# A new order of finds, sorts, deals and indirect transfers, with a sixth of each unit's slots weighted on GpSimd, in a graph attention layer with sparse gathers

## The reference

```python
h = jnp.maximum(_layernorm(x, axis=-1), 0.0)        # x: 8192 x 256
hp = (h @ W.T).reshape(n, 8, 32)
attn = s_src[:, None, :] + s_dst[None, :, :] + adj[:, :, None] * We[:, 0] + be
attn = jnp.where((adj > 0)[:, :, None], attn, -jnp.inf)
attn = softmax(leaky_relu(attn, 0.2), axis=1)
out = x + einsum('ijh,jhd->ihd', attn, hp) + h @ Wr.T + br
```

## Time and profile before

| | us |
|---|---|
| median of 3 timed runs | 2473.1 (2469.73 to 2473.41) |
| span of the profiled execution | 2707.2 |
| VectorE busy | 2058.7 (76%) |
| GpSimd busy | 1627.7 (60%) |
| ScalarE busy | 1264.6 (47%) |
| TensorE busy | 1104.5 (41%) |
| mean rate of all DMA | 180 GB/s |

### The profile page before, as it was taken

How to read it: one execution, slowest core, us unless ns; L and a number is a source line. 1 busy time by engine, 2 the same in 40 slices (tenths; PEclk the granted TensorE clock), 3 DMA queues, 4 the chain that set the end, 5 groups by cost and what they waited for, 6 DMA issues and landing times.

```text
span 2707.2 us, 24949 instructions
## 1 busy us (share of the span) xinstructions
PE 1104.5 (41%) x3781; PEld 826.0 (31%) x3782; DVE 2058.7 (76%) x5510; ACT 1264.6 (47%) x5256; POOL 1627.7 (60%) x1928
## 2 busy tenths in 40 slices
PE   4676003331150237534363336346245344245244
PEld 3554002221140226322152215225134234234123
DVE  5897819983974899757289848989989999997312
ACT  2332002262121336846585556466475464466376
POOL 5444671477265677677537763675774764763774
PEclk9988556665575667666566656666666666666667
DMA  6446752674644676766358764876877787782332
GB/s 151 152 139 212 223 124 81 189 214 120 200 139 141 208 209 192 214 164 189 106 173 251 200 182 152 236 250 194 254 240 226 240 248 232 237 242 55 85 91 57
DMA packets 166650, 488.40 MB, mean 180 GB/s; under 512 B 35744, under 2 KB 54200, under 8 KB 166280
## 3 DMA queue, kind: packets, MB, share of 16 engines
q1 hardware_dynamic: 86088, 278.11, 31.7%
q0 software_dynamic: 80400, 208.74, 29.4%
HBM read 449.88 MB, written 36.83 MB: 180 GB/s over the span
## 4 chain that ended last, share of the span: by engine, by line
DVE 29%; issue 25%; ACT 12%; DMA 12%; POOL 12%; another core or an unknown queue 5%; PE 3%; SPq 1%; POOLq 0%; DVEq 0%; ACTq 0%
ACT arena L1173 10%; POOL arena L596 10%; DVE work L758 8%; DMA arena<-table,arena 7%; DVE work L747 7%; DVE arena L909 2%; DMA out_dram<-w_all,arena 2%; DVE work L804 2%; DVE work L801 2%; DVE work L803 2%; DVE work L800 1%; DMA adj_sb<-in_adj_dram 1%; PE banks L1327 1%; ACT pre L1158 1%
## 5 line engine op out<-in xcount | busy, mean ns | idle before, releaser
L596 POOL DMA_INDIRECT arena<-table,arena x1253 | 1306.0, 1042 | 624.6 <-issue 392.0
L1173 ACT ACTIVATE arena<-arena,prob 128x32 f32<-128x32 f32 x4456 | 1000.4, 308 | 249.5 <-issue 229.4
L1305 PE MATMUL banks<-arena,ident 128*128 128x256 f32 x1392 | 448.3, 495 | 1109.1 <-DVE arena L909 887.1
L1305 PEld LDWEIGHTS banks<-arena,ident 128*128 128x128 f32 x1392 | 350.9, 258 | 1206.1 <-issue 902.5
L747 DVE FIND_INDEX8 work<-work,adj_sb 128x8 uint32<-128x502 f32 (+56 forms) x775 | 670.7, 868 | 0.0
L758 DVE MAX8 work<-adj_sb 128x8 f32<-128x502 f32 (+56 forms) x775 | 659.3, 858 | 0.0
L1311 PE MATMUL banks<-arena,ident 128*128 128x256 f32 x1114 | 381.8, 472 | 376.2 <-remote 255.6
L1168 ACT ACTIVATE prob<-pre 128x120 f32<-128x120 f32 (+21 forms) x67 | 21.7, 323 | 943.2 <-DVE pre L893 710.5
L1311 PEld LDWEIGHTS banks<-arena,ident 128*128 128x128 f32 x1114 | 226.3, 223 | 516.6 <-remote 303.8
L909 DVE TENSOR_TENSOR arena<-arena,prob 128x768 f32<-128x768 f32 (+8 forms) x166 | 200.7, 1258 | 0.0
L1158 ACT ACTIVATE pre<-arena,we_all 128x13 f32<-128x13 f32 (+27 forms) x536 | 170.4, 407 | 51.4 <-DMA arena<-lists 31.6
(11 more groups left out here) (130 smaller groups left out, 1088.0 us busy)
## 6 DMA issues: line engine op xcount, KB each, us to landing
adj_sb<-in_adj_dram SPq DMA_DIRECT2D x505, 512.0 KB, 15.3
arena<-table,arena POOLq DMA_INDIRECT x1253
table<-arena POOLq DMA_DIRECT2D x32, 264.0 KB, 2.6
arena<-in_x_dram SPq DMA_DIRECT2D x32, 256.0 KB, 2.8
resid<-arena POOLq DMA_DIRECT2D x32, 256.0 KB, 2.6
out_dram<-arena POOLq DMA_DIRECT2D x32, 256.0 KB, 2.8
adj_sb<-in_adj_dram SPq DMA_DIRECT2D x1, 1536.0 KB, 22.6
lists<-arena,rank POOLq DMA_INDIRECT x67
```

Of the source, the lines that this page charges most:

```text
L596: pool.indirect_dma_start(gath[:, un.slot(k), :], None, table[:, :], bass.IndirectOffsetOnAxis(ap=rec[:, k, 0:1], axis=0), bounds_check=N ...
L1173: last = s.activation(g, g, ACT.Copy, scale=prob[:, b, k * H + h:k * H + h + 1])
L1305: last = m.matmul(ps_sum[:, u % 2, :], ident[:, :], gath[:, un.slot(k), 0:HD], start=(k == 0), stop=False)
```

## The change

- **Finds:** `FOUND` is now a table of points with steps between them: one find more in step 0, the same from unit 1 to 11, and fewer from unit 12 on (51 instead of 53 at unit 40, 59 instead of 61 at unit 48). The last find is in step 60.
- **Groups:** the last group of 8 becomes two of 4; in all 1262 slots instead of 1253. The deals of groups 4 to 8 move by one to two units; for groups 6, 7 and 8 the deal and the load are now behind the same gather (units 34, 42, 50), ahead of the group's first unit.
- **Homes:** three homes for lists instead of two, with a width for each.
- **Scan and sort:** FIND_INDEX8 comes two segments behind MAX8 instead of one; the low and high halves of the sort wait on semaphores of their own.
- **Indirect DMAs** (gathers, stores, deals) have no `bounds_check`.
- **Weights:** ScalarE takes 2K//5 slots (479 in all instead of 557), GpSimd K//6 from unit 12 on (107 in all), VectorE the rest (676 instead of 696). GpSimd's order is now gather(u), weight(u-2), store(u-3). TensorE adds GpSimd's slots last, and ScalarE's exponentials of unit u wait for GpSimd's weights of unit u-2.

```diff
-          (56, (20, 13, 11, 10, 9, 8, 7, 6)))
+          (56, (20, 11, 9, 8)),
+          (60, (18, 11, 9, 7)))
-FOUND = (7, 9, 10, 11, 14, 16, 18, 20, 21, 22)
-LEAD = 13
+FOUND = ((0, 8), (1, 9), (2, 10), (3, 11), (4, 14), (5, 16), (6, 18), (7, 20), (11, 24), (40, 51), (48, 59), (60, 67))
+HOMES = 3
+POOL_FROM = 12
...
-        self.act_slots = K // 2 if K < 18 else 10 if K < 20 or K > 38 else 14 if K < 32 else 16
+        self.act_slots = 2 * K // 5
+        self.pool_slots = K // 6 if u >= POOL_FROM else 0
...
-                        bass.IndirectOffsetOnAxis(ap=rec[:, k, 0:1], axis=0),
-                        bounds_check=N + PAD - 1, oob_is_err=False).then_inc(lane, 16)
+                        bass.IndirectOffsetOnAxis(ap=rec[:, k, 0:1], axis=0)).then_inc(lane, 16)
+
+            def weight(un):
+
+                n, first = un.pool_slots, un.K - un.act_slots - un.pool_slots
+                pool.wait_ge(S["exped"], un.u + 1)
+                for k, at, n in un.slots(first, first + n):
+                    gv = gath[:, at:at + n, 0:HD].rearrange("p k (h d) -> p k h d", d=D)
+                    pb = prob[:, un.u % 2, k * H:(k + n) * H].rearrange("p (k h) -> p k h", h=H)
+                    last = nc.gpsimd.tensor_tensor(gv, gv, pb.unsqueeze(3).to_broadcast([P, n, H, D]), ALU.mult)
+                last.then_inc(S["pool_weighted"], 1)
...
             for un in units:
                 gather(un)
+                if un.u - 2 >= POOL_FROM:
+                    weight(units[un.u - 2])
                 if un.u >= LATE:
                     store(units[un.u - LATE])
...
+            for un in units[-2:]:
+                weight(un)
...
                     v.max(val8[:, 8 * s:8 * s + 8], a[:, bounds[s]:bounds[s + 1]]).then_inc(S["maxed"], 1)
-                    if s:
-                        index(s - 1)
+                    if s >= 2:
+                        index(s - 2)
                 if end == so.segs:
+                    index(so.segs - 2)
                     index(so.segs - 1)
...
+                for keys_of, top, done in ((kl, sl, S["sorted_lo"]), (kh, sh, S["sorted_hi"])):
+                    if m:
+                        dve.wait_ge(done, sorted_before[c] + m - (c if done is S["sorted_lo"] else 0))
+                    if m % 2 == 0:
+                        v.max(top, keys_of).then_inc(done, 1)
+                    else:
+                        v.match_replace(keys_of, top, keys_of, 0.0).then_inc(done, 1)
...
+                if u - 2 >= POOL_FROM:
+                    act.wait_ge(S["pool_weighted"], u - 2 - POOL_FROM + 1)
...
+                if un.pool_slots:
+                    pe.wait_ge(S["pool_weighted"], u - POOL_FROM + 1)
+                for n in range(un.pool_slots):
+                    k = K - un.act_slots - un.pool_slots + n
+                    last = m.matmul(ps_sum[:, u % 2, :], ident[:, :], gath[:, un.slot(k), 0:HD],
+                                    start=False, stop=(n == un.pool_slots - 1))
                 last.then_inc(S["tile_sum"], 1)
```

More of the change, by code:

```diff
@@ L81 @@
 VMAX = 8 * max([n for n, _ in SEGS.values()] + [len(b) - 1 for b in WINDOW_SEGS])
-WIDE = max(len(ks) * (HEAD + 2 * ks[0]) for ks in LISTS)
+WIDES = [max(len(ks) * (HEAD + 2 * ks[0]) for ks in LISTS[i::HOMES]) for i in range(HOMES)]
 VALID = max(len(ks) * ks[0] for ks in LISTS)
@@ L153, in plan @@
             units.append(Unit(len(units), K, group, i))
-    found = [FOUND[u] if u < len(FOUND) else min(len(sources), u + LEAD) for u in range(len(units))]
+    found = []
+    for u in range(len(units)):
+        (u0, f0), (u1, f1) = next(((a, b) for a, b in zip(FOUND, FOUND[1:]) if a[0] <= u < b[0]), (FOUND[-1], FOUND[-1]))
+        found.append(f0 + (f1 - f0) * (u - u0) // max(1, u1 - u0))
     for group in groups[1:]:
@@ L171, in plan @@
                 owner[un.slot(k)] = ("part_sum", part_sums + n + 1)
-        for k in range(un.K - un.act_slots, un.K):
+        for k in range(un.K - un.act_slots - un.pool_slots, un.K):
             owner[un.slot(k)] = ("tile_sum", un.u + 1)
+        assert not un.u > POOL_FROM or all(
+            not free or free[0] == "part_sum" and free[1] <= units[un.u - 2].parts_before or free[0] == "tile_sum" and free[1] <= un.u - 2
+            for free in un.free_at)
         part_sums += un.parts
@@ L252, in gat_kernel @@
         adj_sb = sb("adj_sb", [P, 2, N])
-        arena = sb("arena", [P, GSLOTS * ROW + 4 * WIDE])
+        arena = sb("arena", [P, GSLOTS * ROW + 2 * sum(WIDES)])
         gath = arena[:, 0:GSLOTS * ROW].rearrange("p (k r) -> p k r", r=ROW)
-        stage, dealt = (arena[:, GSLOTS * ROW + i * 2 * WIDE:GSLOTS * ROW + (i + 1) * 2 * WIDE].rearrange(
-            "p (b w) -> p b w", b=2) for i in range(2))
+        homes = [GSLOTS * ROW + sum(WIDES[:i]) for i in range(HOMES)]
+        stage, dealt = ([arena[:, at + i * sum(WIDES):at + i * sum(WIDES) + width] for at, width in zip(homes, WIDES)]
+                        for i in range(2))
         work = sb("work", [P, max(5 * VMAX + 4 * KMAX, 2 * TILES * D)])
@@ L282, in gat_kernel @@
         rank_f = sb("rank_f", [P, GMAX])
[L283 removed]
+        rank = sb("rank", [P, HOMES, GMAX], U32)
         lower = sb("lower", [P, P])
@@ L394, in record @@
         def record(un):
-            return dealt[:, un.group.g % 2, un.place * un.group.W:(un.place + 1) * un.group.W]
+            return dealt[un.group.g % HOMES][:, un.place * un.group.W:(un.place + 1) * un.group.W]
         def staged(so):
-            return stage[:, so.group.g % 2, so.place * so.group.W:(so.place + 1) * so.group.W]
+            return stage[so.group.g % HOMES][:, so.place * so.group.W:(so.place + 1) * so.group.W]
         def pairs(rec, K):
@@ L625, in deal @@
                     pool.indirect_dma_start(
-                        lists[group.g][:, :], bass.IndirectOffsetOnAxis(ap=rank[:, group.g % 2, i:i + 1], axis=0),
-                        stage[:, group.g % 2, i * group.W:(i + 1) * group.W], None,
-                        bounds_check=group.n * P - 1, oob_is_err=False).then_inc(lane, 16)
+                        lists[group.g][:, :], bass.IndirectOffsetOnAxis(ap=rank[:, group.g % HOMES, i:i + 1], axis=0),
+                        stage[group.g % HOMES][:, i * group.W:(i + 1) * group.W], None).then_inc(lane, 16)
             def load_dealt(group):
                 landed(pool, group.deal_seq + group.n)
-                if group.g >= 2:
-                    before = groups[group.g - 2]
+                if group.g >= HOMES:
+                    before = groups[group.g - HOMES]
                     landed(pool, units[before.first + before.n - 1].store_seq + (2 if before.t0 is None else 1))
@@ L812, in decode @@
                 t, K, rec = so.t, so.K, staged(so)
-                if so.place == 0 and so.group.g >= 2:
-                    before = groups[so.group.g - 2]
+                if so.place == 0 and so.group.g >= HOMES:
+                    before = groups[so.group.g - HOMES]
                     landed(dve, before.deal_seq + before.n)
                 pv = pairs(rec, K).bitcast(U32)
-                dve.wait_ge(S["sorted_"], sorted_before[c] + 2 * so.rounds)
+                dve.wait_ge(S["sorted_lo"], sorted_before[c] - c + 2 * so.rounds - 1)
+                dve.wait_ge(S["sorted_hi"], sorted_before[c] + 2 * so.rounds)
                 v.tensor_scalar(pv[:, :, 0], slot_lo[:, 0:K], JBITS, None, ALU.logical_shift_right)
@@ L1311, in tile_sums @@
                     last = m.matmul(ps_sum[:, u % 2, :], ident[:, :], gath[:, un.slot(k), 0:HD],
-                                    start=False, stop=(k == K - 1))
+                                    start=False, stop=(k == K - 1 and not un.pool_slots))
+                if un.pool_slots:
[4 more added lines that the diff above has]
+                                    start=False, stop=(n == un.pool_slots - 1))
                 last.then_inc(S["tile_sum"], 1)
```

37 lines of the change are left out of this document (14 added, 23 removed).

## The result

The changed kernel takes **2569.1 us** (median of 4 runs, 2567.38 to 2573.05), the kernel before on the same chip 2473.3 (2469.73 to 2476.31): a ratio of 1.0395, with an interval of 1.0379 to 1.0410. It is 96 us slower. I had forecast 2552, a range of 2400 to 2620, and slower. Its profiled execution took 2571.4 us, so this profile can be read as it stands.

The account below looks back on a forecast made before the run. It took VectorE's own work plus its waits to set the end, with GpSimd's gathers bounding 815 to 1334 us. Terms -6 + 157 + 22 - 12 - 27 - 60 + 22 - 17 = +79 on 2473.1 gave 2552 us, range 2400 to 2620.

Parts of the forecast that it names:

- item 4: Sort halves on two semaphores, indices two segments behind, three homes for lists: 0, as VectorE's operations follow without gaps.
- the new order: Lower found counts, last find in step 60: tail 155 instead of 229.6 us, taken as -60; find no longer hidden +22.
- transfers without checks: Indirect transfers at 1.25 us instead of 1.30, over some 340 in the GpSimd-bound stretch: -17.
- shares and weighting as such: Part of item 1: VectorE's 20 fewer slots -6, ScalarE waits replaced -27.
- the lock: weight(u-2) queued behind gather(u), so evacuate(u-2) waits: +157 at group edges, +22 at the start, -12 for replaced gather waits.
- The price at group edges: Behind place() in groups 4 to 8, VectorE waits for deals, loads, gathers and weighting before evacuating: +157 together.
- item 1: GpSimd's weighting from unit 12 on and the order it brings: -6, +157, +22, -12, -27.
- about 155 us behind the last find: Sign for the forecast: a tail of that length, instead of 229.6 us counted from 2477.6.
- ScalarE waits nearly gone: Sign for the forecast: VectorE's waits for ScalarE nearly disappear; the sum subtracted 27 for them.
- (a): Rival: indirect transfers become much cheaper, 1.00 us or less each, so 2399 us, faster; chance 0.20.
- (b): Rival: the order at group edges is covered after all, so item 1's 157 isn't there: 2395 us; chance 0.12.
- (c): Rival: GpSimd's multiplications hold VectorE up or the other way round, at most 68 us again, 2620; chance 0.08.

Follow-up runs that it names:

- the undisturbed one: The kernel before, no edit, profiled a second time, without the first profile's odd spells of waiting: 2477.3 us in a single run, span 2475.6.
- the finds placed anew: Changed kernel with a new FOUND table (more finds by units 6 to 12): 2407.8 us weighting ahead of gathers, 2440.8 behind, 2393.6 without GpSimd weighting.
- the best run: Changed kernel with a new FOUND table (more finds by units 6 to 12) and no weighting on GpSimd: 2393.6 us, ratio 0.9673.

## Why the prediction was right, and where it was not

The runs form a chain from the kernel before to the changed one, one part at a time: 2475 without checks 2420, with item 4 2411, with the shares and GpSimd's weighting ahead 2430, with the new order 2471, with the weighting behind the gathers 2569.

| part | in my sum | measured |
|---|---|---|
| transfers without checks | -17 | -55 (-61 on the changed kernel) |
| item 4 | 0 | -10, intervals overlap |
| shares and weighting as such | -6 - 27 = -33 | +19 |
| the new order | -60 + 22 = -38 | +41 |
| the lock | 157 + 22 - 12 = +167 | +98 (+52 in the old order) |
| together | +79 | +93 |

The measured parts sum to 93 from a base of 2475 to 2476; the result itself is 96 over its own base of 2473. The prices hold for the parts added in this order: the runs show others for the lock and the weighting where the rest differs.

The sign is right, and so is the mechanism of the largest term, the weighting's place behind the gathers. That the forecast came within 17 us is luck: four of five terms are off by 35 us or more, against each other, and the new order, which I had as a gain of 38, is a loss of 41. The steps:

**The price at group edges** was right. I worked out 22 for the start (step 13) and then 10, 23, 3, 38, 27, 28, 28. The trace has 24.9 and then 8.9, 18.8, 4.2, 30.8, 23.9, 25.5, 25.5, with two of 2.0 and 6.6 besides: 171 against 179. Most edges are a little cheaper, as a load and a landing took less than taken from the earlier trace rows (the lists were there 3.50 us after the load, not 6.3).

**What the lock replaces** was the failed step of item 1. I subtracted 12.3 from the earlier trace rows, that is, the gather waits of the kernel before behind 1345. But the lock stands in the new order, and there VectorE waits 280 us for gathers over the whole kernel, of which the lock takes 130 over. Then 214.5 - 4.2 - 130 + 20 (L919, 49.8 against 30.0) = 100, and the medians say 98. Here a wait moved one find ahead cost only what it exceeded the old wait by.

**The new order** failed by a term that I put at nothing, not by those that I had. Behind the last find I had 155 - 32 = 123 us; the changed kernel took 119.5 (2451.9 to 2571.4). (The 155 is counted from the old last find, so my sign "about 155 us behind the last find" was put wrongly.) Against the run with the old order the tail is 94 us shorter (215.6 to 122.1). What it pays is a last find that comes 131 us later (2343 instead of 2211.8): 27 are the six steps from 54 to 60 at 4.5 (I had counted seven), 21 the find that is no longer hidden (22 predicted), 71 are waits for gathers between 1150 and 2211, which I didn't have, and 12 are left over. These waits stand behind the deals, which the lower counts of finds push from three units ahead of a group to right ahead of its first gathers. I had reckoned such edges only for the lock; without the lock the same gathers are late for the scores.

**The transfers.** The period, 1.25, was right. The row that I took it by, the register MOVE of 29 ns, is gone from the trace, but what got shorter is the transfer itself, by 50 ns. That my guess of 1.25 hit it is partly luck. The stretch that they bound was wrong: the earlier trace rows were taken from 815 on, and the gathers ahead of it, and those up to 1580, weren't looked at.

**ScalarE's waits.** I subtracted 27 for them from the execution with the spells. In the undisturbed one they are 26.5, and in the changed kernel they rise to 49.8. The new order raises them: with the same shares and the weighting ahead they are 10.1 in the old order and 30.0 in the new, and the lock takes them to 49.8. Of the things that I said would show the forecast right, "ScalarE waits nearly gone" failed.

**Rivals.** (a) fell: the gap of 0.30 stays. (b) fell: the lumps are there. (c) fell as a price of 68 us, as one slot instead of K//6 costs the same, but what it is about is there. In the changed kernel's timeline of VectorE and GpSimd, an operation of VectorE beside a multiplication of GpSimd, and the same one elsewhere:

```profile
1606.31 1.92 POOL L617 TENSOR_TENSOR arena<-arena,prob 128x1024 f32<-128x1024 f32 x1
1606.61 1.70 DVE L792 SCALAR_TENSOR_TENSOR work<-work,seg_base 128x56 uint32<-128x56 uint32 x1
...
2382.69 0.22 DVE L792 SCALAR_TENSOR_TENSOR work<-work,seg_base 128x56 uint32<-128x56 uint32 x1
```

It takes 1.70 us instead of 0.22 and ends 0.08 us after GpSimd's. What the Trainium skill says in "GPSIMD Engine Reference", section 1 Specifications, of SBUF interfaces shared with VectorE, and of contention with an instruction of two SBUF inputs, agrees with this trace (this one reads work and seg_base). Eleven of VectorE's instructions behind 270 us took over 0.3 us longer than the usual time of their shape; each ran beside such a multiplication, and together they make some 10 us. Six of them have two inputs, four (TENSOR_SCALAR, L819 and L840) only one, and one stood behind one of these, so two inputs aren't the whole condition here. Most of VectorE's find isn't touched: with the weighting ahead, FIND_INDEX8 over 1505 columns takes 1.72 us beside a multiplication, five times, and 1.72 elsewhere.

**GpSimd's multiplications** came cheaper than the 0.63 us a slot that I took from the earlier trace rows. Groups by line:

```profile
L617 POOL TENSOR_TENSOR arena<-arena,prob 128x512 f32<-128x512 f32 x20 | 22.1, 1103 | 24.6 <-ACT prob L1192 24.1
L617 POOL TENSOR_TENSOR arena<-arena,prob 128x768 f32<-128x768 f32 x10 | 15.0, 1496 | 0.2
L617 POOL TENSOR_TENSOR arena<-arena,prob 128x256 f32<-128x256 f32 x21 | 13.8, 657 | 38.9 <-ACT prob L1192 38.6
L617 POOL TENSOR_TENSOR arena<-arena,prob 128x1024 f32<-128x1024 f32 x4 | 7.7, 1924 | 0.1
```

107 slots took 58.6 us, 0.55 each. But GpSimd also waits 62.7 us for ScalarE ahead of them, which was in no term, and VectorE does the same slot in 0.3.

**Open** is what of the 19 us of the shares and the weighting is which; with the finds placed anew the weighting alone costs 14, and in the changed kernel's order nothing clear of noise. ScalarE's new share was tried in no run by itself. Whether the best run is the best order wasn't tried either.

## What to carry to other kernels

Where two engines take turns in bounding a kernel, ask of every moved piece of work two things: what is queued ahead of it in its new place, and what its consumer was already waiting for one step later; the price is the difference, and it depends on the rest of the order (here 98, 52 or 33 us for the same two lines). Count the stretch that an engine bounds from its waits over the whole span, before multiplying a saving per instruction by a number of instructions. An engine that looks 64% busy had little time to give: with the finds placed anew, the kernel is 14 us faster without its multiplications. That fastest version is 3.3% (82 us) faster than the kernel before, and most of it is not the finds: leaving out the bounds checks alone gave 55.

## What the hardware showed

A bounds check on an indirect transfer costs 0.05 us of GpSimd (busy 1.00 instead of 0.95); the gap of 0.30 us to the next one stays. GpSimd's multiplication took 0.66 us for 256 elements per partition, 1.10 for 512, 1.50 for 768 and 1.92 for 1024, so by these figures some 0.2 us and then 1.5 to 1.7 ns for each element; its addition took 1.26 for 512. Small operations of VectorE that ran beside such a multiplication ended with it (1.70 us instead of 0.22), while FIND_INDEX8 kept its time. And one profiled execution of a kernel was 234 us longer than the timed runs, with many short odd waits, where another of the same kernel was not.
